# The second round's first attention, moved into a third stream of the first round

## What is computed

```python
# x (4, 512, 128), ctx_1024 (4, 154, 128); all float32
x = x + tanh(g_xattn[0]) * attention(layernorm(x), ctx, Wq, bq, Wk, bk, Wv, bv)   # "first attention"
x = x + tanh(g_ffn[0])   * local_attention_block(layernorm(x))                    # 2 layers, 8 heads, windows of 64
x = x + tanh(g_xattn[1]) * decoder_layer(layernorm(x), ctx)                       # diagonal self attention, cross attention, MLP
x = x + tanh(g_ffn[1])   * experts(layernorm(x))                                  # 64 routed experts, top 8, and 2 shared
```

## Time and profile before

| what | value |
|---|---|
| median of 3 runs | 874.73 us (873.94 to 876.95) |
| the profiled execution, its own time | 875.49 us |
| its span in the trace | 873.70 us |
| mean granted TensorE clock | 0.906 of 2.4 GHz |
| PE busy | 722.2 us (83%) |
| DVE busy | 548.1 us (63%) |
| ACT busy | 535.9 us (61%) |
| POOL busy | 341.0 us (39%) |
| DMA | 41.83 MB, mean 48 GB/s |

### The profile page before, as it was taken

How to read it: one execution, slowest core, us unless ns; L and a number is a source line. 1 busy time by engine, 2 the same in 40 slices (tenths; PEclk the granted TensorE clock), 3 DMA queues, 4 the chain that set the end, 5 groups by cost and what they waited for, 6 DMA issues and landing times.

```text
span 873.7 us, 15858 instructions
## 1 busy us (share of the span) xinstructions
PE 722.2 (83%) x5368; PEld 470.6 (54%) x5368; DVE 548.1 (63%) x2196; ACT 535.9 (61%) x1345; POOL 341.0 (39%) x384
## 2 busy tenths in 40 slices
PE   5758788897879876778779889869888898889997
PEld 4436465564656645554456465546565564665443
DVE  5776856778645647569757647646666555763623
ACT  4358495775927426456796694795795955554542
POOL 4454524455442445334344334334243234522100
PEclk9788999998987976899979889999899898789999
DMA  7610010100100000211121301200302001004243
GB/s 257 201 44 1 14 43 13 33 13 13 44 13 1 2 1 2 83 41 30 40 65 40 88 19 32 77 8 13 80 26 49 25 26 30 13 16 130 67 133 90
DMA packets 37162, 41.83 MB, mean 48 GB/s; under 512 B 14345, under 2 KB 23771, under 8 KB 36955
## 3 DMA queue, kind: packets, MB, share of 16 engines
q1 hardware_dynamic: 37083, 40.83, 16.8%
HBM read 28.75 MB, written 2.62 MB: 36 GB/s over the span
## 4 chain that ended last, share of the span: by engine, by line
PE 46%; DVE 25%; ACT 16%; POOL 7%; issue 3%; DMA 1%; SPq 0%; DVEq 0%; POOLq 0%; ACTq 0%
ACT work L863 8%; PE act_psum L614 5%; PE moe_psum L624 5%; PE dve_psum L446 4%; PE dve_psum L517 3%; PE act_psum L507 3%; DVE work L1129 3%; DVE res_nrm L1111 2%; PE act_psum L713 2%; PE act_psum L776 2%; DVE stats L1101 2%; POOL work L1518 2%; DVE work L1152 2%; PE dve_psum L716 2%; POOL rstd L1501 2%
## 5 line engine op out<-in xcount | busy, mean ns | idle before, releaser
L1518 POOL TENSOR_TENSOR work<-work,rinv 128x512 f32<-128x512 f32 (+1 forms) x80 | 87.9, 1110 | 146.2 <-DVE rinv L1119 146.0
L863 ACT ACTIVATE work<-work,nbias,rnorm 128x128 f32<-128x128 f32 x256 | 123.5, 485 | 8.5 <-DVE nbias L1192 8.2
L1559 POOL TENSOR_TENSOR hT<-hT,work 128x512 f32<-128x512 f32 x32 | 40.8, 1274 | 82.1 <-DVE work L1152 82.1
L1500 POOL TENSOR_SCALAR rstd<-mv 128x2 f32<-128x2 f32 x72 | 16.9, 234 | 141.4 <-DVE mv L1104 141.4
L446 PE MATMUL dve_psum<-wqkv,hTs 128*128 128x512 f32 x128 | 66.7, 646 | 2.0 <-ACT hTs L1010 2.0
L846 ACT COPY v_loc<-act_psum 77x512 f32<-77x512 f32 (+2 forms) x72 | 41.4, 583 | 33.8 <-PE act_psum L451 16.0
L1129 DVE CUSTOM_DVE_ANT_0 work<-dve_psum,masks 128x128 f32<-128x128 f32 x256 | 58.3, 283 | 3.2 <-PE dve_psum L477 3.1
L433 PE MATMUL act_psum<-ident,res_nrm 128*128 128x128 f32 x96 | 26.4, 365 | 37.6 <-DVE res_nrm L1111 37.5
L846 ACT COPY hT<-act_psum 128x512 f32<-128x512 f32 (+1 forms) x60 | 31.2, 526 | 41.2 <-PE act_psum L507 23.3
L1501 POOL TENSOR_TENSOR rstd<-rstd,neg_half 128x2 f32<-128x2 f32 x72 | 52.3, 726 | 6.0
L1148 DVE TENSOR_TENSOR hT<-dve_psum,tab_a 128x512 f32<-128x512 f32 x32 | 22.1, 690 | 47.0 <-PE act_psum L458 32.4
(11 more groups left out here) (222 smaller groups left out, 2001.2 us busy)
## 6 DMA issues: line engine op xcount, KB each, us to landing
ahead<-cwT_dram SPq DMA_DIRECT2D x128, 64.0 KB, 2.0
v_loc<-v_loc SPq DMA_DIRECT2D x24, 256.0 KB, 3.7
kT<-cwT_dram SPq DMA_DIRECT2D x80, 64.0 KB, 2.0
qT<-cwT_dram SPq DMA_DIRECT2D x48, 64.0 KB, 2.0
wqkv<-in_wqkv_dram SPq DMA_DIRECT2D x2, 768.0 KB
res_nrm<-in_x_dram SPq DMA_DIRECT2D x4, 256.0 KB, 3.0
w_m<-in_w_m_dram SPq DMA_DIRECT2D x1, 1024.0 KB, 8.3
v_loc<-v_loc SPq DMA_DIRECT2D x8, 128.0 KB, 3.2
```

Of the source, the lines that this page charges most:

```text
L863: last = nc.scalar.activation(weights[:, i, :], weights[:, i, :], ACT.Exp, bias=nbias[u][:, b, i:i + 1], scale=scale_of(i), accum_out=sums ...
L1518: nc.gpsimd.tensor_tensor(some, some, by.unsqueeze(2).to_broadcast(list(some.shape)), ALU.mult).then_inc(ready[u], 1)
L1559: nc.gpsimd.tensor_tensor(own, own, partners[u][:, t % 2, k, :], ALU.add).then_inc(turned_ready[u], 1)
```

## The change

The first attention of samples 2 and 3 leaves their slots and becomes the beginning of the third stream, which thus has work in the first round: 8 steps for sample 2 and then 8 for sample 3, ahead of the deferred experts. It works in the experts' idle buffers: x and then its sum in `experts_in`, the normalised x in `units0`, later queries and pieces of probabilities there, keys, the context's transpose and all small statistics in `units1`, the transposed x and later y in `units2`, probabilities, context and values in `ahead0` and `ahead1`. At the end SyncE writes y, x and the context's transpose to DRAM (`first_y_dram`, `first_x_dram`, `first_ctxT_dram`), and in the router steps of sample 0 or 1, once the slot's own hT and x are kept, loads them into the slot's buffers. PE waits for y before the first transpose of the local layer (`ctx_loaded`, 2 x 16) and for the rest where it is used. The wait for `hT_kept` goes from ACT in the first attention to DVE ahead of the first rotation.

The third stream's step stands ahead of a slot's step number 18, 19, 20, 28, 41, 42, 43 and 51, in each slot (`FIRST_AHEAD_OF`): 18 to 20 are the second scores and the first probabilities of the local layer, 28 is the transpose ahead of its MLP, and 41 to 51 are the same places of the second layer. As slot 1 runs 10 steps behind, sample 2's steps 0 to 3 stand ahead of slot 0's steps 18, 19, 20 and 28 and its steps 4 to 7 ahead of slot 1's. The 50 steps of deferred experts are now spread over 138 instead of 154 turns, from the same moment on. Numbers of lines below are those of the changed kernel, 41 and more higher.

```diff
+FIRST_STEPS = 8
+BODY_STEPS = FIRST_STEPS + LAYERS * (1 + 2 * TILES + 2 + TILES + 2 + 6) + 7 + CROSS_STEPS + 7 + 4
...
+FIRST_AHEAD_OF = (18, 19, 20, 28, 41, 42, 43, 51)
 def turns():
-    total = ROUNDS * BODY_STEPS + EXPERT_STEPS
-    out, done, placed = [], [0, 0], 0
+    total = ROUNDS * BODY_STEPS - FIRST_STEPS + EXPERT_STEPS
+    out, done, placed, first = [], [0, 0], 0, 0
     for slot in [0, 1] * TOGETHER + [0] * LEAD + [0, 1] * (total - LEAD - TOGETHER) + [1] * LEAD:
+        if first < DEFER * FIRST_STEPS and done[slot] in FIRST_AHEAD_OF:
+            out.append(len(SLOTS))
+            first += 1
         out.append(slot)
         done[slot] += 1
         begun = done[0] + done[1] - (2 * (BODY_STEPS + 1) - LEAD)
-        while placed < DEFER * DEFERRED_STEPS and placed * 2 * (BODY_STEPS - 2) < begun * DEFER * DEFERRED_STEPS:
+        while placed < DEFER * DEFERRED_STEPS and placed * 2 * (BODY_STEPS - FIRST_STEPS - 2) < begun * DEFER * DEFERRED_STEPS:
             out.append(len(SLOTS))
             placed += 1
...
+        def first_views(own, other):
+            return own[0:DEFER] + [other] * DEFER
+        first_x = first_views(nrm, tokens(e))
+        first_out = first_views(x, tokens(e))
+        first_y = first_views(y, tokens(u2))
...
-                steps.append(chain.from_iterable(deferred_experts(u) for u in range(DEFER)))
+                steps.append(chain(chain.from_iterable(first_steps(u) for u in SAMPLES[DEFER:]),
+                                   chain.from_iterable(deferred_experts(u) for u in range(DEFER))))
...
PE
+                def sample_steps(u):
+                    if u < DEFER:
+                        yield from first_steps(u)
...
-                        transpose_tiles(("hTs", l, u), y, u, LN_OUTER if l == 0 else None)
+                        if u >= DEFER and l == 0:
+                            pe.wait_ge(ctx_loaded[u], 2 * 16)
+                        transpose_tiles(("hTs", l, u), y, u, LN_OUTER if u < DEFER and l == 0 else None)
...
ACT
-                    if u >= DEFER:
-                        act.wait_ge(hT_kept[u - DEFER], 16)
...
DVE
                     if u >= DEFER and l == 0:
                         dve.wait_ge(cwT_stored[u - DEFER], 16)
+                        dve.wait_ge(hT_kept[u - DEFER], 16)
...
-                    if u >= DEFER:
-                        dve.wait_ge(x_kept[u - DEFER], 16)
...
SyncE
+                    sp.wait_ge(first_kept[BATCH - 1], 3 * 16)
                     sp.wait_ge(hT_kept[u], 16)
...
+                def first_steps(u):
+                    if u >= DEFER:
+                        if u > DEFER:
+                            sp.wait_ge(first_kept[u - 1], 3 * 16)
+                        load_sample(sp, u)
+                    for _ in range(FIRST_STEPS - 1):
+                        yield
+                    if u >= DEFER:
+                        sp.wait_ge(ln_done[u], TILES * (LN_OUTER + 1))
+                        sp.dma_start(first_y_dram[u], first_y[u].rearrange("p t d -> p (t d)")).then_inc(first_kept[u], 16)
+                        sp.dma_start(first_x_dram[u], first_out[u].rearrange("p t d -> p (t d)")).then_inc(first_kept[u], 16)
+                        sp.dma_start(first_ctxT_dram[u], first_ctxT[u]).then_inc(first_kept[u], 16)
+                    yield
...
-                        load_sample(sp, u + DEFER)
+                        follower = u + DEFER
+                        sp.wait_ge(first_kept[follower], 3 * 16)
+                        sp.dma_start(flat(y[u]), first_y_dram[follower]).then_inc(ctx_loaded[follower], 16)
                         sp.dma_start(hT_dram[u], hT[u][:]).then_inc(hT_kept[u], 16)
                         sp.dma_start(x_dram[u], flat(x[u])).then_inc(x_kept[u], 16)
+                        sp.dma_start(ctxT[u][:], first_ctxT_dram[follower]).then_inc(x_loaded[follower], 16)
                     sp.wait_ge(act_emptied, act_item["cwT", u] + 1)
                     sp.dma_start(cwT_dram[u], cwT[u]).then_inc(cwT_stored[u], 16)
                     if is_deferred(u):
+                        sp.wait_ge(x_kept[u], 16)
+                        sp.dma_start(flat(x[u]), first_x_dram[follower]).then_inc(x_loaded[follower], 16)
```

141 lines of the change are left out of this document (88 added, 53 removed).

## The result

| | before | changed |
|---|---|---|
| median of the runs, us | 874.98 (872.41 to 878.58, 19 runs) | 881.5 (879.26 to 887.11, 19 runs) |
| ratio | 1 | 1.0084, 95% interval 1.0071 to 1.0097 |
| profiled execution, span, us | 873.7 | 878.9 |

The change costs 7.3 us (the ratio, taken on the kernel before), where 3.6 us of gain were forecast. Of the changed kernel's executions 13 lie at 879.3 to 882.6 us and 6 at 884.6 to 887.1, and some of its variants (e4, e5, e13) show two such groups as well, so that a median of four to six runs moves by 1 to 2 us with how many fall into each.

The account below looks back on a forecast made before the run. PE, busy 722 of 874 us, was taken as the bound, its 151 us idle as what can be won. 873.7 - 18.9 + 14.8 + 0.5 = 870.1 us of span gave a forecast of 871.1 us, range 861 to 881.

Parts of the forecast that it names:

- The likeliest case: Whole kernel: 18.9 us gained at the meeting, 14.8 paid in the first round, 0.5 for DMA; 871.1 us, chance 0.30.
- There remain 64.4 us to compare: Sample 0's router end to sample 3's y transpose: 73.0 us less 8.6 of experts; less 15.0 work, 8.9 waits, leaves 40.5.
- New waits: Meeting of the rounds: sample 2's projections and rotation beside sample 1's end make PE wait 5.0 us, bounds 0 and 10.
- four turns after its load is issued: DMA of y: asked for four turns after issue, so far from use; a 256 KB transfer lands in 3.4 us.
- Steps 6 and 7: First round, DVE: about 4 us of work lies where DVE waits for exponentials, costing 0.1 us per sample.
- Steps 0 to 2: First round: layer norm statistics on DVE exposed, 1.4 us; normalising and copy in idle time, PE transposes 0.9 us; per sample.
- Step 4: First round, ACT: four exponentials ahead of slot 1's eight; with step 5's copy 5.0 us per sample, bounds 1 and 7.
- Steps 3 to 5: First round: queries (step 3) cost nothing; exponentials and the 0.6 us copy in step 5 make 5.0 us per sample.
- the blocked queue: Rival: ACT and DVE stand for third-stream steps while the slot's next instruction is ready; 12.5 to 13 us per sample, 881.8 us, chance 0.24.
- it decides from 9.2 us per sample on: First-round price per sample above which, by the forecast, nothing is gained from the move.
- Only moved work: Rival: a microsecond of PE work costs about 0.76 us wherever it stands; 11.4 us each way, 874.7 us, chance 0.22.

Follow-up runs that it names:

- e4: Changed kernel with steps 6 and 7 of samples 2 and 3's first attention left out on DVE and POOL: 876.42 us, ratio 1.0014 to the kernel before.
- e5: Changed kernel with each of the four exponentials of samples 2 and 3's first attention done on one column: 881.47 us, ratio 1.0088 to the kernel before.
- e13: Changed kernel with four extra matmuls in front of each of PE's two long waits at the meeting of the rounds: 883.31 us, ratio 1.0097.
- e1: Changed kernel with the first attention of samples 2 and 3 left out on all engines: 863.56 us, ratio 0.9873 to the kernel before.
- e2: Kernel before with samples 2 and 3's first attention taken out, eight empty steps in its place: 868.68 us, ratio 0.9933 to the kernel before.
- e9: Changed kernel with the load of the follower's y issued five steps earlier, ahead of the third expert weight fill: 879.94 us, ratio 1.0075.
- e10: Changed kernel with both samples' first attention in slot 0's decoder steps, inputs loaded in an earlier step, y's load early: 876.01 us, ratio 1.0020.
- e12: Changed kernel with ACT's four exponentials of samples 2 and 3's first attention one turn behind the scores: 881.81 us, ratio 1.0079.
- e14: Changed kernel with sample 2's first attention in the decoder, sample 3's at the meeting, deferred experts eight turns later: 871.3 us, ratio 0.9964.
- e16: Like e14, but sample 3's steps three turns later, deferred experts eleven turns later than in the change, y's load one step early: 869.82 us, ratio 0.9930.

## Why the prediction was wrong

The likeliest case gave 3.6 us of gain, and the loss of 7.3 us came out. By the medians the change returned 11.1 us where 18.9 were forecast and cost 18.4 where 14.8 were (e1). The profiled executions put it at 15.6 (150.0 + 362.9 against 132.2 + 365.1) and 19.5, so the gain has some 4 us of play and the cost 1. By either, the change gives back less than forecast and costs more.

- **"There remain 64.4 us to compare", less 15.0 and 8.9: the step that failed most.** It took PE's work and waits of the first attention as time that goes when they go. e2 shows that both samples together cost 5.9 us there. Closing the turns gave another 5.2. In the stretch itself the changed kernel has 5.5 us of the 18.9 (64.4 less 58.9). The reading that e9, e10 and e13 speak for is that the stretch waits for DVE, POOL and ACT anyway and PE's 15 us lay partly in these waits; the granted clock, which fell in e2, may have taken a part.
- **"New waits", 5.0 with bounds 0 and 10.** PE's waits in the stretch are 17.0 us, where 12.4 less 8.9 plus 5.0 would be 8.5. (The three waits of slot 0's lone rotation, from which the 5.0 was taken, are 5.7 us in sum, not about 7.) Of the 8.5 us more, the 5.1 for y's load are a mistake in "four turns after its load is issued": SyncE's own wait at the third fill was not looked up. But e9 shows that this wait was worth 0.8 us. The visible wait and the price are two things.
- **The clock.** TensorE was granted 0.82 there in place of 0.98. It is busy 42.6 us, where 60.5 less the 15.0 moved and the 8.6 of experts would be 36.9, an estimate of 5.7 us for the clock. I had not counted that, and it did not matter there: with 0.95 (e13) nothing is gained. The Trainium skill (TensorE: Matmul & The Clock Gate, Part 1) says that activity of the array releases its throttle; in e13 it did, from 0.82 to 0.95, without a gain in time.
- **Round 1, "Steps 6 and 7: 0.1 us".** Another step that failed: they cost 6.1 us for both samples (e4) where 0.2 were put down. The forecast laid them into DVE's waits for exponentials; at this place the slots' own instructions stand on both sides of the step, and DVE's mean share of 66% does not tell that.
- **Steps 0 to 2, 2.3 us per sample.** Lining up PE's instructions with those of before gives 0.1 us for sample 2 and 4.6 for sample 3. Of the 4.6, 2.9 arise at sample 3's steps 0 and 1 (PE's matmuls ahead of them are 7.0 us late, those behind 9.9), where step 0's copy on ACT at the head of the queue, the exposed table load and PE's bank stand; these were not in the sum. The drain of 1.38 us that the Trainium skill (ScalarE: Activation LUTs, What ACT_TABLE_LOAD costs) adds to a load does not show here either: the load of 177.33 ends at 178.61, the next activation starts at 178.63. Where a trace and that figure differ, the trace decides.
- **Step 4, "the dear one", 5.0 us.** Steps 3 to 5 did delay PE by 4.0 and 4.5 us in that comparison, and ACT's rows look as forecast: the size was nearly right. Of the cause given, ACT's wait found no support (e12 takes it away and gains nothing), and ACT's four exponentials were not tested, since e5 frees too little. What the delay hangs on stays open. (Steps 6 and 7 delay PE by 4.0 and 3.4 us in the same comparison.)
- **The rival that came true,** the blocked queue, was priced at 12.5 to 13 us per sample with the gain at 18.9. Its time (881.8) was hit by luck, with both terms off: 9.2 per sample, and the gain 7.8 smaller. Its rule "it decides from 9.2 us per sample on" holds only for that gain; at 11.1 us the change loses from 5.6 us per sample on.
- **Only moved work,** 0.76 us for each of PE's, was nearer in time (874.7 us) but had one price for all places. At the meeting the first attention cost 0.39 us for each us of its PE work (5.9 of 15, e2), in the first round 1.23 (18.4 of 15, e1). That these two differ, with the 5.2 us of the closed turns, is the result.

## What to carry to other kernels

Before work is moved out of a stretch with waits, ask what the stretch would take without it: leave it out and measure. Here 15 us of PE's work and 8.9 us of its waits were worth 5.9 us where they stood. When moving it, do not go by low mean shares: what counts is what stands ready behind the step on each in-order queue, the DMA queue with its waits among them. A wait that ends at a late transfer may be worth nothing: mending the one of 5.1 us gained 0.8 (e9). And where an arrangement wins (e14 to e16), cut its time into stretches before giving the reason: theirs arose in a stretch that the moved work is not in.

## What had not been expected of the hardware

- Raising TensorE's granted clock from 0.82 to 0.95 over 58 us, with eight matmuls in its waits, moved the time by nothing measurable (e13: ratio 1.0097 against 1.0084).
- A function table load of 1.28 us delays nothing while ACT would wait anyway (165.34 us in the kernel before: ACT still waits 0.43 us behind it), and delays the next activation in full when an instruction ahead of it takes that wait (177.33 us in the changed kernel, with the maxima ready since 175.07). What the five loads less are worth to the whole kernel, no run isolates.
